# One exponent operation on ScalarE for the four heads of a group in place of one for each pair, with the order of the steps written anew

## The reference

```python
x = x + attn(layernorm(x))            # self-attention, 16 heads of 16, rotary q and k, 256 keys
x = x + xattn(layernorm(x), ctx)      # cross-attention, 16 heads of 16, 77 keys
x = x + ffn(layernorm(x))             # a graph of six attention nodes
# in ffn, for c in range(6): 8 heads of 32, 256 keys
#   q, k, v = scaled edge projections of earlier nodes
#   nodes[c] = act_w[c] * (softmax(q' k'^T / sqrt(32)) v') @ Wo[c] + q
#   the result is layernorm(nodes[5]) * ln_g + ln_b
```

## Time and profile before

| | |
|---|---|
| median of 3 executions | 5218.73 us (5194.44 to 5224.57) |
| the profiled execution's own time | 5204.53 us |
| its span, first to last instruction | 5202.7 us, mean granted TensorE clock 0.963 |
| TensorE matmul busy | 4697.6 us (90%) |
| VectorE busy | 3447.5 us (66%) |
| ScalarE busy | 2485.9 us (48%), of it L830 1138.7 us in 1280 operations |
| GpSimd busy | 671.0 us (13%) |

### The profile page before, as it was taken

The page is one execution under the profiler, slowest core; times in us unless marked ns, Lnnn a source line. Parts: engine busy times, 40 slices in busy tenths (PEclk is TensorE's granted clock), DMA queues, the critical chain, the costliest instruction groups (busy, mean ns, idle before and its releaser), DMA issues.

```text
span 5202.7 us, 204839 instructions
## 1 busy us (share of the span) xinstructions
PE 4697.6 (90%) x87132; PEld 2899.1 (56%) x87132; DVE 3447.5 (66%) x5930; ACT 2485.9 (48%) x4737; POOL 671.0 (13%) x1606
## 2 busy tenths in 40 slices
...
DMA packets 43111, 48.29 MB, mean 9 GB/s; under 512 B 11552, under 2 KB 41888, under 8 KB 42144
## 3 DMA queue, kind: packets, MB, share of 16 engines
...
...
## 4 chain that ended last, share of the span: by engine, by line
issue 54%; PE 30%; POOL 6%; DVE 5%; ACT 1%; POOLq 1%; DVEq 0%; ACTq 0%; DMA 0%; SPq 0%
PE banks L967 15%; PE banks L961 14%; DVE row_max L927 2%; POOL neg_max L733 2%; POOL neg_max L735 2%; DVE n_tok L946 1%; POOL inv_std L706 1%; PE banks L1088 1%; POOL x_tok L712 1%; ACT probs L830 1%; DVE k_parts L899 0%; POOL var_eps L703 0%; PE banks L1018 0%; ACT n_tok L759 0%; POOL rope_c L719 0%
## 5 line engine op out<-in xcount | busy, mean ns | idle before, releaser
L927 DVE TENSOR_REDUCE row_max<-banks 128x4 f32<-128x1024 f32 (+1 forms) x1152 | 1300.3, 1169 | 327.5 <-PE banks L961 325.7
L830 ACT ACTIVATE probs<-banks 128x1024 f32<-128x1024 f32 (+1 forms) x1280 | 1138.7, 935 | 512.6 <-PE banks L961 486.1
L961 PE MATMUL banks<-k_parts,q_parts 32*128 32x256 f32 (+1 forms) x13824 | 599.5, 305 | 183.5 <-DVE row_max L927 143.1
L961 PEld LDWEIGHTS banks<-k_parts,q_parts 32*128 32x128 f32 x13824 | 482.2, 196 | 393.6 <-DVE row_max L927 184.0
L961 PE MATMUL banks<-q_parts,k_parts 32*128 32x256 f32 (+1 forms) x13824 | 600.4, 302 | 99.3 <-DVE row_max L927 63.2
L946 DVE TENSOR_TENSOR n_tok<-probs 128x512 f32<-128x512 f32 x512 | 384.8, 752 | 447.7 <-ACT probs L830 372.9
L961 PEld LDWEIGHTS banks<-q_parts,k_parts 32*128 32x128 f32 (+1 forms) x13824 | 462.4, 187 | 327.0 <-issue 117.2
L967 PE MATMUL banks<-node_t,w_n 128*32 128x256 f32 x10240 | 622.0, 381 | 4.7 <-ACT node_t L847 4.7
L733 POOL TENSOR_TENSOR neg_max<-row_max,zeros 128x8 fp32r<-128x8 f32 (+1 forms) x576 | 140.5, 244 | 3659.3 <-DVE row_max L927 3657.0
L946 DVE TENSOR_TENSOR pair_sums<-probs 128x512 f32<-128x512 f32 x512 | 369.1, 721 | 362.6 <-ACT probs L830 185.4
L840 ACT ACTIVATE context_t<-banks 128x256 f32<-128x256 f32 x512 | 197.2, 385 | 582.9 <-PE banks L961 581.1
...
## 6 DMA issues: line engine op xcount, KB each, us to landing
...
```

Of the source, the lines that this page charges most:

```text
L830: done(act.activation(probs[s][0:rows, g % 2, 2 * p:2 * p + 2, 0:kt, :] .rearrange("p c k t -> p c (k t)"), psum[0:rows, b0:b0 + 2, 0:kt * T],
L927: done(dve.reduce_max(maxima, scores, AX_X, negate=True), "max_taken", a)
L961: return nc.tensor.matmul(bank_ap, lhs, rhs, start=start, stop=stop, **kw)
```

## The change

The two EX of a group become one, over four banks: 128 by 2048 elements (77 by 1024 in cross-attention). PV, PS and both PA of the group wait for that one. The banks of ST and SX now come free all four at once. `ORDER` is another text: 882 steps in place of 922, the 40 that are gone being the second EX of each group. All other steps are the same ones, in another sequence for each engine and partly in other banks, and the place of the turn has moved.

```diff
-    if k in ("S", "SB", "ST", "SX"):
-        return [("MX" if k in ("S", "SB") else "EX", s, j, key[3], p) for p in range(2)]
+    if k in ("S", "SB"):
+        return [("MX", s, j, key[3], p) for p in range(2)]
+    if k in ("ST", "SX"):
+        return [("EX", s, j, key[3], 0)]
...
             elif k == "EX":
-                g, p = a[3:]
+                g = a[3]
...
-                b0 = BANK["ST", s, j, g][2 * p]
-                done(act.activation(probs[s][0:rows, g % 2, 2 * p:2 * p + 2, 0:kt, :]
+                b0 = BANK["ST", s, j, g][0]
+                done(act.activation(probs[s][0:rows, g % 2, :, 0:kt, :]
                                     .rearrange("p c k t -> p c (k t)"),
-                                    psum[0:rows, b0:b0 + 2, 0:kt * T],
+                                    psum[0:rows, b0:b0 + 4, 0:kt * T],
                                     ACT.Exp, scale=1.0 / math.sqrt(head_dim(j))), "exp_done", a)
...
-                dve.wait_ge(sem["exp_done"], reached(at, "exp_done", ("EX", s, j, g, p)))
+                dve.wait_ge(sem["exp_done"], reached(at, "exp_done", ("EX", s, j, g, 0)))
...
-                    events.append(("exp_done", emptied_by(old)[BANK[old].index(i) // 2]))
+                    events.append(("exp_done", emptied_by(old)[0]))
```

In PV and PS the second `("exp_done", ("EX", s, j, g, 1))` is gone from the waits in the same way. Of the order, the lines around the turn, first the end of the text and then its beginning:

```diff
@@ the end of ORDER @@
-+QR1.0@6 +EX0.0.3.0 +EX0.0.3.1 +PV0.0.3 +PA0.0.3.0 +PA0.0.3.1 +PS0.0.3 +RC0.0.1 FG1 +QC1.0 FX1 +QS1.0 +QH1.0.1
-+NR0.0.1 +K1.0@1 +KI1.0 +KC1.0 +OB0.0.0@2 +OB0.0.1 +XA0.0 +LNS0.1 STORE1 +XB1.0 +LOADC0 +V0.1@0 +VE0.1 +QL1.0.1
-+K0.1@1 +KR1.0@6 +LOADC1
++PA0.0.3.0 +QR1.0@6 +QS1.0 +PV0.0.3 +K0.1@1 +PS0.0.3 +RC0.0.1 +NR0.0.1 +K1.0@2 +OB0.0.0@7 +OB0.0.1 +QH1.0.1
++KI0.1 +KI1.0 +KC1.0 +XA0.0 +LNS0.1 +QL1.0.1 +V1.0@0 +VE1.0 +KH0.1 +LNP0.1 +LNN0.1 +V0.1@5 +KR1.0@2 +TR0.1@3
++KS1.0 +KL0.1 +TRE0.1 +KH1.0 +VE0.1 +Q0.1@1 +QB0.1 +KL1.0 +QH0.1.0 STORE1 +XB1.0 +XB0.1
@@ the beginning of ORDER @@
-KI0.1 LNP0.1 LNN0.1 KS1.0 V1.0@3 TR0.1@4 KH0.1 KL0.1 TRE0.1 KH1.0 KL1.0 Q0.1@7 QB0.1 VE1.0 QH0.1.0 QH0.1.1
-S1.0.0@0 SB1.0.0 QL0.1.0 QL0.1.1 S1.0.1@4 SB1.0.1 MX1.0.0.0 MX1.0.1.1 MX1.0.0.1 MX1.0.1.0 XB0.1 NM1.0.1 S1.0.2@0
++LOADX0 QH0.1.1 QL0.1.0 QL0.1.1 S1.0.0@4 SB1.0.0 MX1.0.0.1 S1.0.1@0 SB1.0.1 MX1.0.1.1 MX1.0.0.0 MX1.0.1.0
```

LOADC0 and LOADC1, at the end of the text before, stand behind V1.1 in cross-attention of slot 1 after. Other places of the order that the prediction speaks of, TensorE's steps alone, before and after:

```diff
@@ cross-attention, slots 0 and 1 @@
-ST0.1.2 PV0.1.1 PS0.1.1 V1.1 ST0.1.3
+V1.1 ST0.1.2 PV0.1.1 PS0.1.1 ST0.1.3
-ST1.1.0 SX1.1.0 ST1.1.1 SX1.1.1 MT1.1.1 TR0.2 PV1.1.0
+ST1.1.0 SX1.1.0 PV1.1.0 ST1.1.1 SX1.1.1
-S0.2.0 SB0.2.0 PS1.1.2 PV1.1.3 PS1.1.3 S0.2.1
+S0.2.0 SB0.2.0 PV1.1.3 PS1.1.3 K0.3 S0.2.1
@@ nodes @@
-ST0.3.0 SX0.3.0 S1.3.0 SB1.3.0 MT0.3.1 PV0.3.0 ST0.3.1 SX0.3.1 MT1.3.0 PS0.3.0
+ST0.3.0 SX0.3.0 S1.3.0 SB1.3.0 PV0.3.0 MT0.3.1 ST0.3.1 SX0.3.1 K0.5 PS0.3.0
-MT0.4.1 V1.4 S1.4.0 SB1.4.0 PV0.4.0 PS0.4.0 ST0.4.1
+MT0.4.1 S1.4.0 SB1.4.0 PV0.4.0 PS0.4.0 K1.5 ST0.4.1
-ST0.5.0 SX0.5.0 S1.5.0 SB1.5.0 PV0.5.0 ST0.5.1 SX0.5.1 PS0.5.0
+ST0.5.0 SX0.5.0 S1.5.0 SB1.5.0 PV0.5.0 ST0.5.1 SX0.5.1 K0.7 PS0.5.0
-ST0.6.0 SX0.6.0 S1.6.0 SB1.6.0 MT0.6.1 PV0.6.0 ST0.6.1 SX0.6.1 PS0.6.0
+ST0.6.0 SX0.6.0 S1.6.0 SB1.6.0 MT0.6.1 PV0.6.0 ST0.6.1 SX0.6.1 V1.6 PS0.6.0
-ST0.7.0 SX0.7.0 OB1.6.1 MT0.7.1 Q1.7 QB1.7 ST0.7.1
+ST0.7.0 SX0.7.0 MT0.7.1 OB1.6.1 ST0.7.1
@@ self-attention of slot 0, one round ahead @@
-ST1.7.1 SX1.7.1 PV1.7.0 PS1.7.0 V0.0 S0.0.0 SB0.0.0 S0.0.1 SB0.0.1 OA1.7 S0.0.2 SB0.0.2 MT0.0.0 PV1.7.1 S0.0.3
+ST1.7.1 SX1.7.1 PV1.7.0 PS1.7.0 S0.0.0 SB0.0.0 V0.0 S0.0.1 SB0.0.1 PV1.7.1 PS1.7.1 S0.0.2 SB0.0.2 MT0.0.0 OA1.7 OB1.7.0 S0.0.3
-SB0.0.3 OB1.7.0 PS1.7.1 ST0.0.0 SX0.0.0 OB1.7.1 ST0.0.1
+SB0.0.3 ST0.0.0 SX0.0.0 OB1.7.1 MT0.0.1 TR1.0 ST0.0.1
```

More of the change, by code:

```diff
@@ L153 @@
[L153 to L167, removed]
@@ new lines @@
+ST0.1.3@4 XA1.0 LNS1.1 LNP1.1 LNN1.1 NR0.1.0 KL1.1 SX0.1.3 PV0.1.2@3 EX0.1.3.0 TR1.1@0 TRE1.1 PS0.1.2 PV0.1.3
+PS0.1.3 RC0.1.1 NR0.1.1 Q1.1@1 QB1.1 QH1.1.0 QH1.1.1 S1.1.0@4 QL1.1.0 SB1.1.0 MX1.1.0.1 MX1.1.0.0 OB0.1.0@3
+OB0.1.1 QL1.1.1 XA0.1 LNS0.2 NM1.1.0 LNP0.2 MT1.1.0@1 S1.1.2@4 SB1.1.2 MX1.1.2.0 MX1.1.2.1 NM1.1.2 MR1.1.0
+ST1.1.0@0 SX1.1.0 EX1.1.0.0 LNN0.2 PV1.1.0@1 ST1.1.1@4 SX1.1.1 TR0.2@2 MT1.1.1@3 EX1.1.1.0 PS1.1.0 ST1.1.2@4
+MR1.1.1 SX1.1.2 PV1.1.1 TRE0.2 Q0.2@0 EX1.1.2.0 PS1.1.1 K0.2@2 RC1.1.0 QB0.2 ST1.1.3@4 SX1.1.3 KH0.2 NR1.1.0
```

117 lines of the change are left out of this document (62 added, 55 removed).

## The result

| | median us | range us | ratio to before, 95% interval |
|---|---|---|---|
| before, 19 executions | 5213.31 | 5194.44 to 5228.70 | |
| after, 19 executions | 5224.45 | 5216.00 to 5230.90 | 1.0022 [1.0012, 1.0031] |

The change makes the kernel 11 us slower. The forecast was 35 us faster; its range and "within 1%" hold the result, its sign doesn't. So the two traces differ by 25.6 us of span where the medians differ by 11, and a round by 1.3 us (318.3 to 319.6 on average between the starts of KR1.0 in successive rounds).

A forecast was written before the change was run, and what follows sets the result against it. TensorE was taken to bound the kernel, with its idle time as what counts. Turn -33, c_t -7 and distances +5 gave -35 us against 5204.5: 5170, or 5184 for the median; range 5115 to 5245.

The forecast's parts named there:

- within 1%: Whole kernel: the result differs from before by under 1% (52 us), chance 0.53.
- The operation: Exponent on ScalarE: one takes 1.87 us against the pair's 1.94; the rest of ScalarE's saving costs or brings nothing.
- (a) PS, through PA: Sums PS wait for both additions, 3.4 us behind SX instead of 2.8; the new order covers it, cost 0.
- later halves bind: Rival: PA and VectorE work behind it in attentions and nodes, 0.85 us per tight PS; six give 5266; chance 0.13.
- (b) Banks and row maxima: Steps taking over banks wait 1.6 us more a round, those needing row maxima 1.3 less: +5 us over 16 rounds.
- The turn: Where engines fetch the order's beginning: fetches lie beside other engines' work, gain 2.2 us a turn, 33 over 15.
- SyncE and GpSimd: Loads and XB0.1 move; nothing of the chain is behind XB0.1 on GpSimd but NM1.0.1: 0; c_t loads: -7 us.
- c_t wait: LOADC0 and LOADC1 are issued in cross-attention, so TensorE's 6.7 us wait for c_t goes: -7 us.
- a gain of 2: Terms other than the turn: -7 us for c_t and +5 for the distances.
- The rival that it recovers: Clock behind the turn, 0.72: shorter idleness saves a third of the loss, 60 us more, 5124; chance 0.17.
- the drop only behind Q0.1: By the Trainium skill's rule the clock drops some us after the turn, behind Q0.1; gain then as summed.

The follow-up runs named there:

- run 1: Kernel before with one exponent for each group, at the place of the first of the two, order otherwise untouched: 5248.61 us, ratio 1.0062.
- run 11: Kernel before with pairs of exponents kept, half 0 first and the second always directly behind it: 5239.99 us, ratio 1.0052.
- run 10: Run 8's order with one exponent for each group, EX0.7.0 placed as in run 7: 5200.47 us, ratio 0.9966.
- run 8: Run 3 with FG0 and what follows it on GpSimd moved behind the first maxima of the next self-attention: 5159.33 us, ratio 0.9897.
- run 7: Run 1 with EX0.7.0 moved behind NE1.6.0 and NE1.6.1 on ScalarE: 5238.13 us, ratio 1.0036.
- run 2: Kernel after in its new order, each exponent split into two adjacent ones of half a bank group: 5243.68 us, ratio 1.0053.
- run 3: Kernel before with only the turn moved, from ahead of KI0.1 to behind QH0.1.0, pairs kept: 5173.23 us, ratio 0.9913.
- run 4: Kernel after with the turn moved back ahead of KI0.1 (XB1.0 then also clear of LNN0.1), one exponent kept: 5243.55 us, ratio 1.0052.
- run 6: Kernel after with STORE1 and XB1.0 moved ahead of LNP0.1, so XB1.0 no longer runs beside LNN0.1: 5196.99 us, ratio 0.9967.
- run 5: Kernel after with FG0 and what follows it on GpSimd moved behind the first row maxima, away from KL0.0: 5210.13 us, ratio 0.9991.
- run 9: Kernel after with the moves of runs 5 and 6 together: 5189.26 us, ratio 0.9947.
- run 12: Run 8 with XB0.1 also moved behind NM1.0.0 on GpSimd, pairs kept: 5156.74 us, ratio 0.9892.

## Why the prediction was wrong

**The operation**: right in its time (1.87 forecast, 1.88 measured), wrong in "costs or brings nothing". The prediction looked at who waits for `probs`, and not at who waits for something that ScalarE does between the two halves. Such steps stand in 6 of 40 groups (NE1.6.1, RC1.7.0, QH0.3 and others), and in 23 the second half comes first. Runs 1 and 11 show what that is worth in the order before, 0.5 to 0.6%, and run 10 against run 8 0.7%; runs 7 and 10 show one of the steps each. In the new order the term is not what failed: there the single operation is 0.3% faster than the pair (run 2).

**(a) PS, through PA: 0.** Right. PS1.7.0's wait even went from 1.40 us to 0 (FG0 no longer slows its addition), PS0.0.2 and PS0.0.3 together wait 1.3 us as against 1.4, and in the nodes TensorE idles for 7.1 us a round against 8.2. The rival "later halves bind" put its price there and has nothing for it; the halves that bind are those of run 1, another place.

**(b) Banks and row maxima: +1.6 and -1.3 us a round.** The steps named are those that the trace shows: ahead of PV1.1.0 TensorE idles 1.20 us (forecast shortfall 1.1), PV0.3.0 1.12 (1.15), PV0.5.0 1.34 (1.15), MT0.6.1 and PV0.6.0 0.84 (0.85), ST0.7.1 0.70 (0.8). ST1.1.1, S0.2.1, S0.0.3 and ST0.4.1, named as shorter, went from 1.0 to 1.2 each to 0, ST0.0.0, named as longer, from 1.03 to 2.46. Over all named steps the exponent's part came out at some +1 us and the maxima's at -2.9, better than forecast. Not on the list were waits for other work of VectorE and ScalarE, which the reckoning left out, giving no reason: OB1.1.1 (+0.7, the third collision), MT0.2.0 (+0.7) and PV1.7.0 (+0.9), the last two for VE on ScalarE, and some 1 us for the query parts (QH, QL). They use up what the maxima gave.

**The turn: -2.2 us.** The size holds, and is even larger: 3.2 us by the ratio in the order before (run 3), 2.8 in its trace at the first maximum, and as much in the new order (run 4 against run 6). Two things in it are not as told. TensorE hardly idles less, its matmuls run at half clock less often. And LNN0.1 was taken at its old duration, 0.73 us, so after lost two thirds of the gain again (29 us, run 6) to the collision with XB1.0.

**SyncE and GpSimd: 0.** This is the step that failed: it was worth 39 us. It asked what stands behind XB0.1 on GpSimd's own queue, and left out what GpSimd does to VectorE, and FG0 and XB1.0 altogether, which the new order moves beside KL0.0 and LNN0.1. Runs 5, 6 and 9: 16, 29 and 39 us. With them away, the change is 28 us faster than before, against the 35 forecast; the sign of the sum hung on this term. That 28 lies so near to 35 is in part luck. An estimate from the ratios: the turn gave 44 us where 33 was forecast, and the rest of the new text, the c_t wait included, cost some 11 (run 4's 27 less the 16 of FG0) where a gain of 2 was forecast; together 33 us of gain, near the 28 measured. The c_t wait of 7 us went as forecast.

**The clock.** The rival that it recovers did not come true as told. At the turn it moved: V1.0 ran for 3.4 to 4.0 us in all 14 turns before (in 9 of them at a mean clock of 0.55 to 0.65, in 5 at full clock with a second pause of 0.8 to 1.4 us inside it), 2.0 in run 3, while the scores behind now get 0.68 where they got 0.64; the mean over the execution is 0.961 against 0.963. In run 6 the mean rose from 0.959 to 0.967; in run 5, where a wait of the same kind was taken away, the profiled execution has 0.953. What decides that, no run here isolates. The prediction also expected the drop only behind Q0.1; but V1.0, directly behind the stall, was at half clock in 9 of 14 turns before, and Q0.1 in 4.

**Left open.** Runs 8 and 12 are not told apart. By how much the third collision slows the kernel was not tried. Nor was the order of run 10 with RC1.7.0 ahead of EX1.7.1, which would show how much of the 1.1 us a round that TensorE idles longer in self-attention goes with it, nor what the clock and the shorter chain each give.
